# A macaron block with two routed expert stages: the table of tiles read into registers by steps of its own, and every engine's order written anew

## What is computed

```python
x = L0_attn_x
x = x + 0.5 * _L0_ffn_ref(_layernorm(x))   # int8-quantized 128x128 product
x = x + _L0_attn_ref(_layernorm(x))        # conv, gated linear recurrence, gated MLP
x = x + 0.5 * _L0_ffn_ref(_layernorm(x))
x = x + 0.5 * _L1_ffn_ref(_layernorm(x))   # shared expert + top 2 of 8 experts
x = x + _L1_attn_ref(_layernorm(x))        # gated state recurrence
x = x + 0.5 * _L1_ffn_ref(_layernorm(x))   # the same expert layer again

def _expert(x, Wg, Wu, Wd):
    return silu(x @ Wg.T) * (x @ Wu.T) @ Wd.T
def _L1_ffn_ref(x):                        # H = 128, I = 256, 8 experts, top 2
    probs = sigmoid(x @ Wr.T + rb)
    scores, idx = top_k(probs, 2)
    return shared(x) + sum(scores[k] * expert[idx[k]](x) for k in range(2))
```

## Time and profile before

| | |
|---|---|
| median of 3 runs | 793.06 us |
| span of the profiled execution, first to last instruction | 692.3 us |
| difference, what lies around the span | 100.8 us |
| PE busy | 600.1 us, 87% |
| DVE busy (VectorE) | 497.2 us, 72% |
| ACT busy (ScalarE) | 387.7 us, 56% |
| POOL busy (GpSimd) | 419.3 us, 61% |
| moved by DMA | 100.97 MB, mean 146 GB/s |
| chain that ended last | PE 43%, DVE 13%, DMA 9%, issue 6% |

### The profile page before, as it was taken

How to read it: one execution, slowest core, us unless ns; L and a number is a source line. 1 busy time by engine, 2 the same in 40 slices (tenths; PEclk the granted TensorE clock), 3 DMA queues, 4 the chain that set the end, 5 groups by cost and what they waited for, 6 DMA issues and landing times.

```text
span 692.3 us, 14370 instructions
## 1 busy us (share of the span) xinstructions
PE 600.1 (87%) x4124; PEld 476.3 (69%) x4124; DVE 497.2 (72%) x1721; ACT 387.7 (56%) x1019; POOL 419.3 (61%) x445
## 2 busy tenths in 40 slices
PE   0366999999989998999897899999999999978974
PEld 0224565655666797888696686769879989857863
DVE  7997999978998865557224798989877766553335
ACT  2395968988766545444353728466565355533541
POOL 5276696488567777567643614553776575775552
PEclk9996999999999999999999999999999999999997
DMA  7999000001033355666768600124216556566796
GB/s 258 410 411 371 0 1 1 1 0 32 13 99 94 97 156 161 186 193 180 211 176 245 235 6 1 35 66 131 74 43 172 153 151 177 161 182 189 231 297 232
DMA packets 60125, 100.97 MB, mean 146 GB/s; under 512 B 10288, under 2 KB 28592, under 8 KB 59792
## 3 DMA queue, kind: packets, MB, share of 16 engines
q1 hardware_dynamic: 50832, 81.52, 38.5%
q0 software_dynamic: 8640, 17.84, 7.4%
q10 hardware_dynamic: 576, 0.69, 0.3%
HBM read 61.79 MB, written 38.23 MB: 144 GB/s over the span
## 4 chain that ended last, share of the span: by engine, by line
PE 43%; DVE 13%; DMA 9%; issue 6%; POOL 3%; SPq 2%; ACT 2%; POOLq 0%; DVEq 0%; ACTq 0%
PE bank L1083 13%; PE bank L1058 6%; PE bank L1296 5%; DMA tin<-rows_by_expert 3%; PE bank L969 3%; PE bank L955 3%; PE bank L944 2%; DMA hid<-rows_done 2%; DMA rows_done<-tout,tdst 2%; PE bank L1064 2%; DMA rows_done<-tout,tin 1%; POOL rows_by_expert L840 1%; DVE qt L417 1%; PE bank L312 1%; PE bank L307 1%
## 5 line engine op out<-in xcount | busy, mean ns | idle before, releaser
L840 POOL DMA_INDIRECT rows_by_expert<-xx,sidx x128 | 128.1, 1001 | 72.2 <-issue 34.0
L1083 PE MATMUL bank<-tint,twt 128*128 128x128 f32 x1136 | 151.8, 282 | 6.0 <-DVE thidt L1121 3.4
L1083 PEld LDWEIGHTS bank<-tint,twt 128*128 128x128 f32 x1136 | 141.1, 196 | 22.0 <-issue 12.3
L1132 POOL DMA_INDIRECT rows_done<-tout,tin x98 | 96.3, 983 | 57.5 <-ACT tout L1107 34.8
L1121 DVE TENSOR_TENSOR thidt<-tsil,bank 128x256 f32<-128x256 f32 x142 | 58.2, 418 | 95.8 <-ACT tsil L1099 74.1
L1099 ACT ACTIVATE tsil<-bank 128x256 f32<-128x256 f32 x142 | 53.9, 384 | 89.9 <-PE bank L1083 88.4
L1058 PE MATMUL bank<-e_dn,thidt 128*128 x568 | 90.6, 286 | 15.5 <-DVE thidt L1121 7.3
L1058 PEld LDWEIGHTS bank<-e_dn,thidt 128*128 128x128 f32 x568 | 76.8, 195 | 25.2 <-issue 24.8
L1107 ACT ACTIVATE tout<-bank,tin 128x128 f32<-128x128 f32 x142 | 50.2, 366 | 62.9 <-PE bank L1064 43.7
L1132 POOL DMA_INDIRECT rows_done<-tout,tdst x44 | 43.7, 993 | 49.0 <-ACT tout L1107 35.9
L1296 PEld LDWEIGHTS bank<-bufA,bufB 128*127 128x127 f32 (+6 forms) x448 | 47.7, 176 | 11.6 <-issue 6.7
(11 more groups left out here) (272 smaller groups left out, 1331.0 us busy)
## 6 DMA issues: line engine op xcount, KB each, us to landing
twt<-moe_gu SPq DMA_DIRECT2D x142, 256.0 KB
rows_by_expert<-tout SPq DMA_DIRECT2D x25, 715.0 KB, 20.0
tin<-rows_by_expert SPq DMA_DIRECT2D x142, 65.0 KB, 2.6
hid<-rows_done SPq DMA_DIRECT2D x12, 512.0 KB, 5.5
x<-x_in SPq DMA_DIRECT2D x8, 256.0 KB, 4.4
rows_by_expert<-xx,sidx POOLq DMA_INDIRECT x128
out<-x SPq DMA_DIRECT2D x8, 256.0 KB, 3.9
rows_done<-tout,tin POOLq DMA_INDIRECT x98
```

The costliest lines, as they stand in the source:

```text
L840: pool.indirect_dma_start(out=rows_by_expert, out_offset=bass.IndirectOffsetOnAxis(ap=sidx[h][:, k:k + 1], axis=0), in_=xx[h][:, r, t, :], ...
L1083: m = pe.matmul(bank[UP_BANKS[p][j]][:, c * P:(c + 1) * P], weights[:, c * P:(c + 1) * P], tint[g % TURNS][:, :], start=True, stop=True)
L1132: pool.indirect_dma_start(out=rows_done, out_offset=bass.IndirectOffsetOnAxis(ap=dst, axis=0), in_=tout[:, g % RING, :], in_offset=None).t ...
```

## The change

`CHUNK` goes, and with it the loads inside the three steps. Two steps of their own come, one on SP and one on PE, each for up to IDS = 16 entries of one wave. The wait on the table is in them; the wait on the scatters (`s_scat`) stays with the first tile of a wave.

```diff
-CHUNK = 4
+IDS = 16
...
-        def chunk_at(j):
-
-            w = wave_of(j)
-            if (j - WAVE_START[w]) % CHUNK:
-                return None
-            return range(j, min(j + CHUNK, WAVE_START[w + 1]))
+        def ids_of(w, k):
+
+            return range(WAVE_START[w] + IDS * k, min(WAVE_START[w] + IDS * (k + 1), WAVE_START[w + 1]))
...
+        def t_ids_sync(sp_, p, w, k):
+            sp_.wait_ge(s_table, WAVES * p + w + 1)
+            row_at.update(values_of(ENG.SP, rtab[p], ids_of(w, k), TOP_ROW))
+            expert_sp.update(values_of(ENG.SP, etab[p], ids_of(w, k), E_ROUTED))
+
+        def x_ids_tensor(pe, p, w, k):
+            pe.wait_ge(s_table, WAVES * p + w + 1)
+            expert_pe.update(values_of(ENG.PE, etab[p], ids_of(w, k), E_ROUTED))
+
         def t_load_sync(sp_, p, j):
             g, w = p * NT + j, wave_of(j)
-            if chunk_at(j):
-                if j == WAVE_START[w]:
-                    sp_.wait_ge(s_table, WAVES * p + w + 1)
-                    sp_.wait_ge(s_scat[0], SCAT * (PAIRS * p + (WAVE_UNITS[w] + 1) // 2))
-                    sp_.wait_ge(s_scat[1], SCAT * (PAIRS * p + WAVE_UNITS[w] // 2))
-                row_at.update(values_of(ENG.SP, rtab[p], chunk_at(j), TOP_ROW))
+            if j == WAVE_START[w]:
+                sp_.wait_ge(s_scat[0], SCAT * (PAIRS * p + (WAVE_UNITS[w] + 1) // 2))
+                sp_.wait_ge(s_scat[1], SCAT * (PAIRS * p + WAVE_UNITS[w] // 2))
...
         def t_weights_sync(sp_, p, j):
             g = p * NT + j
-            if chunk_at(j):
-                sp_.wait_ge(s_table, WAVES * p + wave_of(j) + 1)
-                expert_sp.update(values_of(ENG.SP, etab[p], chunk_at(j), E_ROUTED))
...
-                if chunk_at(j):
-                    pe.wait_ge(s_table, WAVES * p + wave_of(j) + 1)
-                    expert_pe.update(values_of(ENG.PE, etab[p], chunk_at(j), E_ROUTED))
                 pe.wait_ge(s_thid, g + 1)
```

The step lists of all engines are new too: the same steps with the new ones among them, in another order in some hundreds of places. Two lines of the hundreds:

```diff
-            for j in range(2, 4):
+            t_ids_sync(sp_, 0, 0, 0)
...
-            t_weights_sync(sp_, 0, 58)
+            t_ids_sync(sp_, 1, 1, 0)
```

More of the change, by code:

```diff
@@ L1679, in _ @@
                 t_weights_sync(sp_, 1, j)
-            for j in range(57, 59):
+            for j in range(55, 58):
                 t_load_sync(sp_, 1, j)
@@ L2081, in _ @@
             g_level_vector(dve, 0, 0)
+            for j in range(64, 67):
+                x_dst_vector(dve, 0, j)
             g_level_vector(dve, 1, 0)
@@ L2276, in _ @@
             x_dst_vector(dve, 1, 49)
-            for j in range(48, 51):
+            for j in range(48, 50):
                 x_hid_vector(dve, 1, j)
@@ L2403, in _ @@
             q_root_gpsimd(pool, 3, 1)
-            for j in range(0, 2):
+            for j in range(0, 3):
                 t_store_gpsimd(pool, 0, j)
@@ L2407, in _ @@
             q_bias_gpsimd(pool, 7, 1)
[L2408 to L2409 removed]
+            t_store_gpsimd(pool, 0, 3)
             r_scatter_gpsimd(pool, 4, 0, 0)
@@ L2461, in _ @@
             r_scatter_gpsimd(pool, 0, 1, 3)
-            for j in range(69, 71):
+            for j in range(67, 71):
                 t_store_gpsimd(pool, 0, j)
@@ L2779, in _ @@
             e_up_tensor(pe, 5, 0, 1)
             r_turn_tensor(pe, 7, 0)
-            x_io_tensor(pe, 0, 26)
+            x_up_tensor(pe, 0, 23)
+            for j in range(25, 27):
+                x_io_tensor(pe, 0, j)
             e_down_tensor(pe, 5, 0)
@@ L3016, in _ @@
             g_turn_tensor(pe, 7)
-            for j in range(7, 9):
-                x_io_tensor(pe, 1, j)
             e_up_tensor(pe, 3, 1, 0)
@@ L3108, in _ @@
             x_up_tensor(pe, 1, 27)
-            x_io_tensor(pe, 1, 29)
+            for j in range(29, 31):
+                x_io_tensor(pe, 1, j)
             r_turn_tensor(pe, 6, 1)
@@ L3483, in _ @@
             x_out_scalar(act, 0, 25)
-            for j in range(26, 29):
+            for j in range(28, 30):
                 x_silu_scalar(act, 0, j)
@@ new lines, in _ @@
+            for j in range(34, 38):
+                x_silu_scalar(act, 0, j)
+            for j in range(38, 40):
+                x_in_scalar(act, 0, j)
+            for j in range(33, 36):
+                x_out_scalar(act, 0, j)
+            for j in range(40, 42):
+                x_in_scalar(act, 0, j)
+            x_out_scalar(act, 0, 36)
+            x_silu_scalar(act, 0, 38)
+            e_silu_scalar(act, 7, 0, 0)
+            for j in range(39, 41):
+                x_silu_scalar(act, 0, j)
@@ new lines, in _ @@
+            for j in range(42, 44):
+                x_out_scalar(act, 0, j)
+            x_silu_scalar(act, 0, 45)
+            x_in_scalar(act, 0, 48)
+            x_silu_scalar(act, 0, 46)
+            x_in_scalar(act, 0, 49)
+            x_out_scalar(act, 0, 44)
+            for j in range(47, 49):
+                x_silu_scalar(act, 0, j)
+            x_in_scalar(act, 0, 50)
+            for j in range(45, 47):
+                x_out_scalar(act, 0, j)
+            x_in_scalar(act, 0, 51)
+            for j in range(49, 51):
@@ new lines, in _ @@
+            x_silu_scalar(act, 1, 54)
+            x_out_scalar(act, 1, 53)
+            x_silu_scalar(act, 1, 55)
+            x_in_scalar(act, 1, 58)
+            x_silu_scalar(act, 1, 56)
+            for j in range(54, 56):
+                x_out_scalar(act, 1, j)
+            x_in_scalar(act, 1, 59)
+            for j in range(57, 59):
+                x_silu_scalar(act, 1, j)
+            x_out_scalar(act, 1, 56)
+            for j in range(60, 62):
+                x_in_scalar(act, 1, j)
@@ L3898, in _ @@
+            for j in range(59, 61):
                 x_silu_scalar(act, 1, j)
@@ L3927, in _ @@
                 x_silu_scalar(act, 1, j)
-            for j in range(68, 71):
+            for j in range(69, 71):
                 x_out_scalar(act, 1, j)
+            e_silu_scalar(act, 7, 1, 1)
 def kernel(**inputs):
```

1958 lines of the change are left out of this document (963 added, 995 removed).

## The result

| | before | after |
|---|---|---|
| median of 4 runs each, in turn on one chip | 793.40 us | 820.41 us |
| ratio of after to before, 95% interval | | 1.032 (1.0278 to 1.0361) |
| profiled execution: time, span | -, 692.3 us | 818.55 us, 816.8 us |

The change made the kernel slower by 3.2%. The forecast was 791.0 us with a range up to 799: wrong in sign and outside its range.

What follows compares the result with a forecast made beforehand. The prediction took TensorE (PE), busy 87% of the span, to bound the kernel. PE net +3.4, SP net -4.2 and order net -1.3 sum to -2.1 us on 793.1, giving 791.0 us; range 781 to 799.

Steps and rivals of the forecast that it cites:

- 100.8 us around the span: Whole kernel: measured time taken as the 692.3 us span plus 100.8 us around it, giving the median of 793.06.
- Price of a load of 16: Each new long register load: 3.3 us on SP and 3.8 us on PE, from a rising cost per entry.
- The one row that disagreed: Profile row of four entries read from entry 4 in 0.303 us; taken to hint at a fast form at multiples of four.
- What leaves PE and SP: Old loads removed: 9.1 us of gaps go on PE, and seven loads on the chain, 6.2 us, go on SP.
- What comes on PE: PE stops for its new loads, 3.0 us per load of 16: 6.5 in pass 0, 6.0 in pass 1, 12.5 together.
- What comes on SP: SP's two table reads, 6.6 us a step, delay weights by 1 us each at waves 2 and 4 of pass 0.
- In pass 1 it lies in waits for scatters: SP's 6.6 us of table reads in pass 1 fall where SP waits anyway, so nothing was charged.
- All other moves I cost at nothing: Remaining reordered steps only trade places among steps that are both ready: zero, with noise of some 3 us either way.
- The end of the kernel: Products come first, so VectorE's wait for unit 1 and PE's 3.01 us stop go: 3.0 - 1.3 = 1.7 us won.
- End of pass 0: Four 512 KB fetches instead of two ahead of tile 64's weights: 3.4 us, about half hidden, so +1.7.
- Loads of 16 are cheap: Rival: long loads cost only 1.0 to 1.7 us, so the kernel takes 780 to 784 us; chance 0.27.
- SP's block starves PE: Rival: reads ahead of weights of tiles 25 and 45, waves 2 and 4 of pass 0, make 799 us; chance 0.25.

Runs made afterwards that it cites:

- a_again: The change itself, unaltered, run again on another chip: 723.64 us, 1.0584 of the kernel before on the same chip.
- b_aligned: The kernel before, with each wave's part of both tables begun at a column that is a multiple of four: 675.69 us, ratio 0.9899.
- a_chunk4: The changed kernel's order on all engines, with the old loads of four back inside the tiles' steps: 706.96 us, 1.032 of the kernel before.
- chips A: The four chips, taken together, on which the kernel before takes 683 us (682.7 to 683.6 in the median).
- the mixtures: Loads of four, orders switched at about 385 us: new then old 691.57 us (1.0146), old then new 698.51 us (1.0222), against the kernel before.
- b_again: The kernel before, unchanged, profiled once more: 684.78 us, ratio 1.0013, span 684.2 us.
- b_nobias: The kernel before with GpSimd's eight adds of the output bias cut to four columns, on chip B: 794.01 us, ratio 0.9974.

## Why the prediction was wrong

- **"100.8 us around the span": wrong.** The time is the span plus 1.8 us. The 100.8 are a difference between two chips. Since the sum only adds a change of -2.1 to the median, this shifted nothing in it, but it should have told me that the trace of before did not show where 100 us of the measured time were spent.
- **Price of a load of 16: right.** 3.3 to 3.5 us and 3.8 to 4.2 us measured in after (up to 3.7 on SyncE in a_again), 3.3 and 3.8 forecast. The one row that disagreed (0.303 us) was read rightly too: started at a multiple of four, fours take 0.30 us in b_aligned and not 0.87, and no long load but the first wave's had such a start. What I missed is that one could give it to all.
- **What leaves PE and SP (-9.1 and -6.2): not measured by itself.** No run takes the old loads away. b_aligned shortens nearly all 114 of them by 0.6 to 0.7 us, two thirds of their length, and wins 7.7 us, half of those 15.3: no sign against them.
- **What comes on PE (+12.5): nearly right for the stops, but they bring more than their length.** In a_again TensorE's matmuls stood 0.92, 3.05, 2.91, 1.32, 2.92 and 2.83 us behind the six loads of 16, where I had 3.0 for each that counts. With the shorter loads it is 7.6 us in pass 0 (forecast 9.8, or 6.5 after a third was let go) and 7.8 in pass 1 (forecast 6.0; wave 4, which I let count nothing, has 2.8 of them), together 15.4. What the forecast put at nothing is the rest of the +16.7 us that the loads cost against -0.8 forecast. Between the traces of a_chunk4 and a_again, 18.9 us apart, TensorE's stops that end in nothing the profile shows grow from 9.6 to 18.6 us, those that end in a DMA from 7.7 to 14.3, and the same 4,124 records are busy 612.0 us instead of 603.0, at a mean clock of 0.946 instead of 0.964; other waits shrink.
- **What comes on SP (+2): wrong.** The step that failed is "In pass 1 it lies in waits for scatters". SyncE's block made TensorE wait 2.67 us at wave 2 and 3.34 at wave 4 of pass 1, on top of TensorE's own stop and not beneath it, and 3.4 us at wave 4 of pass 0, where I had 1; in the old order SyncE's long loads alone cost 15.6 us. No load was to be on the chain; in a_again SyncE's loads are 3.3% of the span there, some 24 us.
- **"All other moves I cost at nothing, ... some 3 us either way": wrong, and the largest miss.** They cost 23.5 us on chips A: by the mixtures 9 ahead of the end of pass 0's tiles and 16 behind, of which 7 to 9 are the adds. The cause of the first 9 and of what is left behind stays open. I had looked for moves that make something late, not for moves that set work of two engines side by side where one holds the other up (3.28 us for an operation of 0.15); GpSimd's list wasn't looked at for it.
- **The end of the kernel (-1.7): half right.** As forecast, the wait for unit 1 is gone and VectorE's adds run through, 708.33 to 720.3 us in a_again, 12 us after the last product (forecast 12.4). But from TensorE's last tile to the end it is 17.3 us there and 16.1 in b_again: nothing is won at that place, where the row of adds now stands last.
- **End of pass 0 (+1.7): a stop is there, the net is not.** In a_again the weights of tile 64, asked for from 380.5 us on behind four fetches, let its gate product start at 386.58 us, after 3.97 us without a matmul (4.0 in a_chunk4 too; the profile names no releaser, so that it is the fetches fits the place and isn't shown). But from tile 58 to the first level product it is 34.1 us in b_again, 34.3 in a_chunk4 and 32.7 in a_again: other stops that the old order has there are gone.
- **The rivals.** *Loads of 16 are cheap* fell with the price. *SP's block starves PE* was a right mechanism: at wave 4 of pass 0 it struck as named, though through rows and not weights; at wave 2 of pass 0 TensorE stood for its own load alone, and it struck at waves 2 and 4 of pass 1, which it didn't name. With its 799 us it was too small as well, since neither it nor any rival had the order's own loss.

## What to carry to other kernels

- Before longer pieces are made of many small register loads, look where the fast small ones stand: placing the tables so that each piece starts at a multiple of four entries won 1.0% here (0.30 us for four entries in place of 0.87), and longer pieces won nothing beyond that (679.46 us with aligned pieces of 16 against 675.69 with four, in the old order).
- An engine order that is made anew moves work beside other work. Price it by pairs of engines of which one holds the other up (here VectorE's operation of 0.15 us took 3.28 beside two adds of GpSimd), not only by what comes late; before a longer stretch is called a loss, count whether it holds more work; and test the order with the old loads before the new loads are put in.
- Check that the trace's span and the measured time belong together before anything is added up.

## What the runs showed of the hardware that was not expected

**Chips differ.** The kernel before takes 683 us on each of four chips (679 to 689 in 40 runs) and 795 us on chip B (786 to 803 in 25). Up to 228 us of b_again's span the same matmuls start within 3 us of each other in b_again and in b_nobias, the old order on chip B; then, with the tiles, chip B falls behind, by 50 us at b_again's 401 us and 112 at its 647 us. On chip B the waits have rows of a kind that those of chips A don't (first b_nobias; us in total, times, longest), and they are in the waits of after as well:

```profile
ACT tsil L1099 <- remote: 41.0, 12, 7.5
...
ACT tout L1107 <- remote: 27.8, 7, 8.7
DVE bufA L1313 <- remote: 21.2, 6, 5.7
```

```profile
ACT tsil L1096 <- remote: 36.4, 10, 6.6
DVE bufA L1310 <- remote: 13.4, 6, 4.6
```

Counted from the last matmul's end or that of ScalarE's own last work, whichever is later, ScalarE reads a tile's products 0.04 us later, in the median of both traces. Over the 142 tiles that time sums to nothing in b_again (-0.7 us; the matmuls' ends are modelled) and to 45.5 us in b_nobias. Of these 41.4 fall on the 41 tiles with two or more indirect transfers issued between 1.5 us ahead of the end and the read. In b_again 41 tiles have as many and lose nothing. (A long wait has room for more transfers, so this is a sign and no proof.) In order of time, b_nobias:

```profile
597.10 1.06 PE L1083 MATMUL bank<-tint,twt 128*128 128x128 f32 x8
...
599.57 0.96 POOL L840 DMA_INDIRECT rows_by_expert<-xx,sidx  x1 [0.30 <-issue]
...
600.84 0.96 POOL L1132 DMA_INDIRECT rows_done<-tout,tin  x1 [0.30 <-issue]
603.27 0.43 DVE L1313 TENSOR_TENSOR bufA<-bufA,tseg 128x256 f32<-128x256 f32 x1 [5.72 <-remote]
603.46 0.38 ACT L1099 ACTIVATE tsil<-bank 128x256 f32<-128x256 f32 x1 [7.54 <-remote]
```

TensorE had finished those products by 598.2 us; VectorE and ScalarE start 1.5 and 1.7 us after the last of a row of indirect transfers, four of them since 597 us. So part of the 820 us is most likely this, and of the 793 too, whose chip has left no trace of before. Why one chip does it and four others don't was not found out; a kernel that spaces the indirect transfers was not tried.

**TensorE's clock.** The granted clock of after is 0.909 in the mean, against 0.946 for the same kernel on chips A and 0.975 for b_again, and TensorE is busy 640.1, 612.0 and 598.1 us with the same 4,124 records. Behind the 2.83 us stop of a_again the clock is 1.00 and eight records of L1080 take 1.13 us. Behind the 3.34 us stop that comes next it is 0.50 and the eight take 2.05, so this stop cost at least 0.9 us more than its own length:

```profile
662.92:664.97 2.05, 2.05 (x10) 2.05 (x10) 0.00 (x0) 0.00 (x0) 0.00 (x0) 0.50 0.90 240
```
